# Splitting seven routed down blocks instead of five, with part of the low halves on VectorE

## The reference

```python
topk_idx, topk_w = _router(x, gate_w, e_bias)      # 6 of 32 experts, in 4 of 8 groups
combine = zeros((T, 32)).at[arange(T)[:, None], topk_idx].add(topk_w)
h = square(relu(einsum('th,eih->tei', x, up_w)))   # 32 experts x 64
h = h * combine[:, :, None]
moe_out = einsum('tei,ehi->th', h, down_w)
shared = square(relu(x @ shared_up_w.T)) @ shared_down_w.T
out = x + layernorm(moe_out + shared)
```

## Time and profile before

| | |
|---|---|
| median of 3 runs | 501.53 us (501.43 to 502.6) |
| profiled execution | 502.27 us, its span 500.4 us |
| busy: PE | 460.5 us, 92% |
| busy: DVE | 390.0 us, 78% |
| busy: ACT | 354.2 us, 71% |
| busy: POOL | 248.1 us, 50% |
| mean granted PE clock | 0.989 |

### The profile page before, as it was taken

One profiled execution on the slowest core, in us unless ns is written; L12 is line 12 of the kernel. 1 busy time (PEld: TensorE's weight loads), 2 busy tenths in 40 slices (PEclk: granted clock), 3 DMA queues, 4 the chain that ended last, 5 costly groups with the idle time before them and its releaser, 6 DMA issues.

```text
span 500.4 us, 10661 instructions
## 1 busy us (share of the span) xinstructions
PE 460.5 (92%) x3328; PEld 266.2 (53%) x3328; DVE 390.0 (78%) x1000; ACT 354.2 (71%) x707; POOL 248.1 (50%) x583
## 2 busy tenths in 40 slices
PE   2457999999999999999999899999999999999994
PEld 2212444444444454454456566666666666666662
DVE  3688888899999989989648678695977869496453
ACT  2324788888888888888676677768688776866552
POOL 7045323335757835322733617748293764626351
PEclk9999999999999999999899899999999999999998
DMA  7543344444455445430043344455362545546431
GB/s 207 164 144 102 101 132 133 138 137 143 128 148 151 150 124 151 121 101 3 3 175 126 107 151 133 168 182 182 106 213 87 167 155 189 176 114 207 128 104 42
DMA packets 49047, 67.45 MB, mean 135 GB/s; under 512 B 3808, under 2 KB 35808, under 8 KB 48992
## 3 DMA queue, kind: packets, MB, share of 16 engines
q1 hardware_dynamic: 48992, 66.78, 42.4%
HBM read 51.17 MB, written 15.20 MB: 133 GB/s over the span
## 4 chain that ended last, share of the span: by engine, by line
PE 75%; DVE 10%; issue 7%; POOL 4%; ACT 3%; DMA 0%; POOLq 0%; DVEq 0%; ACTq 0%
PE pO L1295 10%; PE pS L1235 9%; PE pY L1376 8%; PE pS L1376 8%; PE pS L1360 6%; PE pS L1362 6%; PE pS L1361 6%; DVE mneg L953 5%; PE pS L1241 3%; PE pX L1220 2%; PE pY L1312 2%; PE pY L1324 2%; PE pX L1223 2%; DVE q_rest L933 1%; PE pX L1215 1%
## 5 line engine op out<-in xcount | busy, mean ns | idle before, releaser
L953 DVE TENSOR_REDUCE mneg<-pS 128x2 f32<-128x512 f32 x256 | 162.2, 685 | 16.5 <-PE pS L1235 16.1
L742 ACT ACTIVATE probs<-pS 128x512 f32<-128x512 f32 x256 | 141.4, 596 | 26.9 <-PE pS L1241 25.4
L1235 PE MATMUL pS<-qk 48*128 48x256 bf16 x512 | 87.6, 289 | 14.9 <-DVE mneg L953 8.4
L827 ACT ACTIVATE h_ring<-r 128x512 f32<-128x512 f32 x104 | 64.5, 625 | 35.7 <-DVE r L1084 27.4
L1360 PE MATMUL pS<-qk,up_hi 128*128 128x512 f32 x144 | 88.7, 616 | 0.0
L1241 PE MATMUL pS<-qk 51*128 51x256 bf16 x512 | 86.6, 280 | 0.5 <-ACT probs L742 0.3
L1295 PE MATMUL pO<-probs,vv 128*32 128x256 f32 x1024 | 72.9, 392 | 0.0
L1235 PEld LDWEIGHTS pS<-qk 48*128 48x128 bf16 x512 | 33.7, 96 | 65.9 <-DVE mneg L953 44.9
L1084 DVE SCALAR_TENSOR_TENSOR r<-pS,probs 128x512 f32<-128x512 f32 x64 | 43.6, 689 | 29.1 <-PE pS L1362 28.1
L1362 PE MATMUL pS<-qk,up_lo 128*128 128x512 f32 x144 | 57.2, 397 | 0.0
L1361 PE MATMUL pS<-qk,up_hi 128*128 128x512 f32 x144 | 57.0, 396 | 0.0
(11 more groups left out here) (191 smaller groups left out, 819.3 us busy)
## 6 DMA issues: line engine op xcount, KB each, us to landing
c_ring<-c_scratch SPq DMA_DIRECT2D x32, 512.0 KB, 4.0
probs<-c_scratch SPq DMA_DIRECT2D x32, 512.0 KB, 3.9
qk<-qk_scratch SPq DMA_DIRECT2D x64, 192.0 KB
qk_scratch<-q_parts SPq DMA_DIRECT2D x16, 192.0 KB, 2.3
qk_scratch<-k_parts SPq DMA_DIRECT2D x16, 192.0 KB, 2.7
qk_scratch<-q_parts SPq DMA_DIRECT2D x16, 128.0 KB, 2.7
qk_scratch<-k_parts SPq DMA_DIRECT2D x16, 128.0 KB, 2.3
out_x<-probs SPq DMA_DIRECT2D x7, 256.0 KB, 4.7
```

The costliest lines, as they stand in the source:

```text
L742: nc.scalar.activation(probs[j][:, hh], s2_bank(n)[:, :, :], ACT.Exp, scale=SCALE).then_inc(exp_done, 1)
L827: nc.scalar.activation(h_ring[:, (n - at) % HRING], r_sb[n % URING][:, :], ACT.Square).then_inc(sq_done, 1)
L953: nc.vector.tensor_reduce(mneg[u % 2][:, :, hh, k], pS1[n % S1_RING][:, :].rearrange("p (a s) -> p a s", a=TH), AX.X, ALU.max, negate=True ...
L1235: return mm(pS1[n % S1_RING][:, T * th:T * (th + 1)], qp[slot][rows, k, P * th:P * (th + 1)], kp[slot][rows, k, :], start=True, stop=True)
```

## The change

Seven routed blocks are split, every second from 2 to 14. Their high parts use a ring of four (the fourth in a tile that attention has left), the whole ones too. The low parts of blocks 2, 6, 10, 14 are made by POOL, in a ring of two. Those of blocks 4, 8, 12 are made by DVE (`low_h`), in a ring of three of their own, behind the rects of k = 8, 11 and 14 (and behind the routing step of the same k). ACT no longer waits for the low part before it writes the whole square. `split_down` is seven blocks wide.

```diff
-SPLIT = (2, 5, 8, 11, 14)
-SPLIT_LAG, HI_RING, LO_RING = 6, 3, 2
+SPLIT = (2, 4, 6, 8, 10, 12, 14)
+SPLIT_LAG, HI_RING, LO_RING = 6, 4, 2
+
+LOW_AT = {8: 1, 11: 3, 14: 5}
...
+        h_lo2 = unit_tail[1:3]
...
                 if i == 0:
-                    low(i, 1)
                     low(i, 2)
                 if i + 1 < NTILE:
                     root_of_sum(i + 1)
                 if i >= 1:
-                    low(i, 1)
+                    low(i, 2)
                 if i + 2 < NTILE:
                     chain_x1(i + 2)
-                if i >= 1:
-                    low(i, 2)
+                low(i, 4)
                 if i >= 1:
                     chain_f(i - 1)
-                low(i, 3)
-                low(i, 4)
+                low(i, 6)
...
-                    if at >= HI_RING:
-                        act.wait_ge(lo_done, at - HI_RING + 1)
-                    elif at == 1:
+                    if at == 1:
                         act.wait_ge(pv_done, 4 * NB)
...
+            def low_h(i, s):
+                n = FBLK * i + SPLIT[s]
+                at, turn = splits_to(n), PER[1] * i + s // 2
+                dve.wait_ge(hi_done, at + 1)
+                dve.wait_ge(sq_done, n + 1)
+                if turn >= len(h_lo2):
+                    dve.wait_ge(split_done, low_user(1, turn - len(h_lo2)))
+                nc.vector.tensor_tensor(h_lo2[turn % len(h_lo2)], h_whole[at % HI_RING], h_hi[at % HI_RING].bitcast(F32),
+                                        ALU.subtract).then_inc(lo2_done, 1)
...
                     if i + 1 < NTILE and k in ROUTE_AT[i >= 1]:
                         route(rt, i + 1, ROUTE_AT[i >= 1].index(k))
+                    if k in LOW_AT:
+                        low_h(i, LOW_AT[k])
...
-                pe.wait_ge(lo_done, at + 1)
-                high, low = h_hi[at % HI_RING], h_lo[at % LO_RING]
+                turn = PER[s % 2] * i + s // 2
+                pe.wait_ge((lo_done, lo2_done)[s % 2], turn + 1)
+                high, low = h_hi[at % HI_RING], (h_lo, h_lo2)[s % 2][turn % LO_RING]
```

More of the change, by code:

```diff
@@ L201, in block_kernel @@
         spare = probs[4][:, :, :, :].rearrange("p a b c -> p (a b c)")
-        h_whole = [h_ring[:, HRING], spare[:, 0:TILE], spare[:, TILE:2 * TILE]]
-        h_hi, h_lo = ([sb(f"{name}{i}", [P, TILE], F32R)[:, :] for i in range(n)]
-                      for name, n in (("h_hi", HI_RING), ("h_lo", LO_RING)))
+        spare2 = probs[5][:, :, :, :].rearrange("p a b c -> p (a b c)")
+        h_whole = [h_ring[:, HRING], spare[:, 0:TILE], spare[:, TILE:2 * TILE], spare2[:, 0:TILE]]
+        unit_tail = [qk[slot][:, half:half + UB // 2].rearrange("p j a b -> p (j a b)").bitcast(F32R)
+                     for slot, half in ((4, 0), (4, UB // 2), (5, 0))]
+        h_hi = [sb(f"h_hi{i}", [P, TILE], F32R)[:, :] for i in range(HI_RING - 1)] + unit_tail[0:1]
+        h_lo = [sb(f"h_lo{i}", [P, TILE], F32R)[:, :] for i in range(LO_RING)]
+        h_lo2 = unit_tail[1:3]
         down_hi, down_lo = (sb(f"down_{n}", [P, len(SPLIT), D], F32R) for n in ("hi", "lo"))
-        down_whole = down_sb[:, :, :].rearrange("p (a b) d -> p a b d", b=3)[:, 0:len(SPLIT), 0]
+        down_whole = down_sb[:, :, :].rearrange("p (a b) d -> p a b d", b=2)[:, 0:len(SPLIT), 0]
         fT_sb = sb("fT_sb", [P, TILE])
-        assert all(k - SBLK == 3 * s for s, k in enumerate(SPLIT))
+        assert all(k - SBLK == 2 * s for s, k in enumerate(SPLIT))
         assert (HRING + 1) * TILE == RBLK * P and TILE >= SI
@@ L300, in block_kernel @@
         sq_done = sem("sq_done")
-        hi_done, lo_done = sem("hi_done"), sem("lo_done")
+        hi_done, lo_done, lo2_done = sem("hi_done"), sem("lo_done"), sem("lo2_done")
         split_done = sem("split_done")
@@ L332, in splits_to, with low_user @@
             return len(SPLIT) * i + sum(at < k for at in SPLIT)
+        PER = {0: len(SPLIT[0::2]), 1: len(SPLIT[1::2])}
+        def low_user(own, turn):
+            i, s = divmod(turn, PER[own])
+            return len(SPLIT) * i + 2 * s + own + 1
         def part3(eng, wait, b):
@@ L621, in low @@
                 n = FBLK * i + SPLIT[s]
-                at = splits_to(n)
+                at, turn = splits_to(n), PER[0] * i + s // 2
                 pool.wait_ge(hi_done, at + 1)
                 pool.wait_ge(sq_done, n + 1)
-                if at >= LO_RING:
-                    pool.wait_ge(split_done, at - LO_RING + 1)
-                nc.gpsimd.tensor_tensor(h_lo[at % LO_RING], h_whole[at % HI_RING], h_hi[at % HI_RING].bitcast(F32),
+                if turn >= LO_RING:
+                    pool.wait_ge(split_done, low_user(0, turn - LO_RING))
+                nc.gpsimd.tensor_tensor(h_lo[turn % LO_RING], h_whole[at % HI_RING], h_hi[at % HI_RING].bitcast(F32),
                                         ALU.subtract).then_inc(lo_done, 1)
```

## The result

| | before | after |
|---|---|---|
| median | 501.98 us (501.43 to 502.6, 4 runs) | 509.05 us (507.67 to 509.87, 4 runs) |
| profiled execution, its span | 502.27 us, 500.4 us | 507.67 us, 505.8 us |
| busy PE, DVE, ACT, POOL | 460.5, 390.0, 354.2, 248.1 us | 456.9, 406.0, 363.8, 247.7 us |
| mean granted PE clock of the profiled execution | 0.989 | 0.956 |

A forecast was written before the change was run, and what follows sets the result against it. TensorE's own stream was taken to set the pace. Tile 0 +0.8, tiles 1 to 5 +6.3, tiles 6 and 7 -0.7 give +6.4 us: span 506.8, time 507.9 us, range 503.0 to 513.0.

The forecast's parts named there:

- 16 x 0.17: TensorE, two more split down blocks in each of 8 tiles, 0.69 us each against 0.86 whole: 2.7 us less.
- The steps: TensorE's uneven steps in a tile: step 10 starts at 16.38 us and wants block 4's low part at 17.94.
- the wait of 1.6 us: TensorE waiting for VectorE's low part of block 4, 17.94 to 19.54: +1.26 us a tile in tiles 1 to 5.
- The port: VectorE's low part of block 4, blocked by GpSimd's h_lo, ends at h_lo's end plus 0.68 less 0.14: 19.46 us.
- The 28.8 us named for tiles without routing: A sign: the tile takes 30.4 us in tiles 1 to 5 and 28.8 without routing.
- Tile 0: First feed-forward tile, low part 4 behind routing step 5: +0.8 us (+1.9 if L1047 is still slowed), half-clock stretch counted equal.
- the 3.5 named as a sign: TensorE's single wait in tile 0 on the VectorE subtraction, claimed to be near 3.5 us.
- Rival (c): TensorE's waits also bring the clock down, 1.7 us each in two to five tiles: 511.3 to 516.4 us; chance 0.18.
- The sum: Whole kernel: +0.8 +6.3 -0.7 = +6.4 us, span 506.8, time 507.9 us.
- (a): Rival: block 4's low part is there by 17.94, no TensorE wait; -2.7 us, 498.8 us; chance 0.07.
- (b): Rival: VectorE's low part starts before h_lo; wait 0.68 us, +0.34 a tile, 503.3 us; chance 0.13.
- Edits at no cost: ScalarE's added squares, later low parts, GpSimd, DMA, rings and wider split_down: 0 taken, 0.9 us at most for split_down.

The follow-up runs named there:

- at7: Changed kernel with VectorE's low part of block 4 one place earlier, behind rect(7) instead of rect(8): 503.89 us, ratio 1.0036 to the kernel before.
- lag7: Changed kernel with all split downs one step later (lag 7) and f copied at k=3 instead of k=2: 505.63 us, ratio 1.0065 to the kernel before.
- pool_after_dve: Changed kernel with GpSimd's h_lo of block 6 waiting until VectorE's low part of block 4 is done: 506.89 us, ratio 1.0086 to the kernel before.
- the repeated run: The changed kernel once more, nothing edited: 509.86 us (507.46 to 510.21), ratio 1.014 to the kernel before.

## Why the prediction was right

**What bounds the kernel.** Right: TensorE's stream sets the pace. Without VectorE's low parts the kernel got 2.6 us faster, against 2.7 worked out from 16 x 0.17. That the two are so near is in part luck: tiles 1 to 5 gave 0.22 us each and not 0.34, and tile 0 made up for it with a half-clock stretch that isn't there.

**The steps.** Tile 4 begins at 377.63 in the changed kernel. Forecast and measured from there: rect(7) 15.48 and 15.43; end of L1055 15.15 and 15.10; rect(8) 17.26 and 17.22; `h_lo` ends 18.92 and 18.86; TensorE wants the low part at 17.94 and 17.93; it goes on at 19.54 and 19.46. So the wait of 1.6 us is 1.53 by starts. The margin by which GpSimd is first was 0.23 and 0.22. The tile grew by 1.26 us (29.11 to 30.37 over five tiles), forecast 1.26: 6.3 us of the sum. That it was read from starts, not from shares, made this possible: the shares show 5 us in 28 free on VectorE.

**The port.** The low part of block 4 takes 1.59 to 1.60 us in tiles 1 to 5, by the formula (end of `h_lo` plus 0.68 less 0.14) 1.59: 396.49 + 0.54 - 395.44. The rule of the Trainium skill ("SBUF — State Buffer", "SBUF: two separate sides") names exactly this pair, a VectorE operation with two SBUF inputs and a GpSimd operation that reads SBUF, and the trace agrees. The part of the rule on GpSimd operations of any width didn't show for a VectorE operation that starts beside a small one: in tile 6 the low part (455.25) took its 0.68 us in the middle of the pow of 128x4 (454.78 to 455.80), and the tile took 27.35 us, 0.33 less than before, forecast 0.34. (The 28.8 us named for tiles without routing was wrong as a length: tile 6 took 27.68 before.) The other way round it did show: in at7, where VectorE's low part starts 0.14 us ahead of the same pow (391.43, 391.57), the pow takes 1.43 us instead of 1.02.

**Tile 0: the term that was mis-sized.** Forecast +0.8; in the profiled execution tile 0 ended 0.7 earlier, apart from 0.47 us that the attention part brought along. The step up to the end of the wait was right (L1055 takes 0.29 at 274.26; TensorE goes on at 275.63 and is through split 6, at up block 13, by 279.37, where it was at 277.8 before: 1.1 later if 0.47 is taken off, forecast 1.0). But I had counted the half-clock stretch behind it as equal, and it isn't there: 278.15 to 281.57 has a granted clock of 1.00 (the 2.4 GHz level), where it had 0.50. That gives back the 1.7 us, and 1.1 - 0.17 - 1.7 = -0.8 is near the -0.7 measured. The wait of TensorE there is 2.56 us, longer than the 2.10 of before but not near the 3.5 named as a sign: TensorE reached it later, in part because it had stood 0.5 us for ScalarE's `onT` at 270.80. So the length of a wait doesn't settle the clock: lag7 waits only 1.88 us there and has 0.51 from 276 to 278 us, and pool_after_dve has a wait of about the same length as the changed kernel (2.57 us), and its clock fell:

```profile
277.00:280.00 3.00, 3.00 (x10) 2.40 (x9) 2.96 (x8) 1.91 (x4) 2.81 (x7) 0.63 0.42 145
280.00:283.00 3.00, 3.00 (x10) 1.75 (x10) 1.80 (x4) 1.55 (x3) 2.62 (x6) 0.80 0.08 30
```

By the Trainium skill ("TensorE: Matmul & The Clock Gate", "What's actually happening") the gate is driven by recent activity in a window that runs on its own; a difference between two runs with the same wait would fit that, and no run here shows more. Rival (c), that the five waits of 1.4 us bring the clock down, did not come true in any profile of these kernels.

**The sum.** In spans: +0.47 (attention) - 0.73 (tile 0) + 6.32 (tiles 1 to 5) - 0.33 - 0.31 (tiles 6, 7) = +5.4, from 500.4 to 505.8. What the +0.47 comes from stays open: `split_down` is 0.8 us longer, and the granted clock is 0.66 in the first 60 us (1.00 before, with the same 35.9 us of busy TensorE); neither was tested. The medians moved by 7.1. The profiled execution is the fastest of the four of its kernel (507.67 us; median 509.05), and its trace can't say where the others lose 1.4 us. The mean clocks on record give a hint: in the repeated run, of those with a mean near 0.95, the one at 0.956 took 507.46 us and those at 0.951 and 0.950 took 509.95 and 510.21. 0.005 of 508 us is 2.5 us of clock, or 5 us at half clock (an estimate from these means), which would fit a stretch like the one of tile 0 that the two profiled executions lack; no trace of a slower execution shows it. That the 507.9 is within 1.2 us of the median is in part luck: the forecast span, 506.8, is 1.0 above the profiled one, because tile 0 was forecast too long, and the median is above the profiled execution.

**Rivals.** (a), the low part is in time: no. (b), the port doesn't bite: no, but its wait is that of a real kernel: in pool_after_dve, where the low part takes 0.68 us, a wait of 0.63 by starts is left (395.59 + 0.86 to 397.08; 0.47 by the modelled end), where (b) had 0.68. Its time isn't: 506.89 us and not 503.3, as the tile there is 0.7 us longer than before and not 0.34.

**Edits at no cost.** split_down's subtraction took 2.11 us, 0.55 more (forecast 0.6); nothing waited for it. The low parts of blocks 8 and 12 made no wait; in tile 4 they ended at 22.9 and 26.5 us of the tile, ahead of the estimated 24.1 and 27.3, as both took 0.68 us. What I hadn't seen: `low_x` (L1088), untouched by the change, took 1.33 us instead of 0.68 beside the `h_lo` of block 10. It was wanted late enough. A slip in the section on the change: the ring of VectorE's low parts (`unit_tail[1:3]`) holds two, not three; both engines count it by twos, and no number used it.

## What to carry to other kernels

Before work is moved to an engine with free time, read at which microsecond its result will be there and at which it is wanted: 5 us in 28 were free on VectorE, and at the one place that mattered the result was about 0.5 us too late before any contention. Where two engines share a port, the order of two starts 0.05 to 0.2 us apart decides over 0.4 to 1.1 us of the follower, and an edit elsewhere (here one square less on ScalarE) can turn it: list what may run beside each blocked operation, and repair with a wait that fixes the order or with another owner of the work. Taking a wait away seldom gives all of it: 3.0 of 4.5 us were gained in one experiment here, where the moved operation blocked another one, and 6.0 of 7.7 in another, where the engine was late for the next thing.

## What the runs showed of the hardware

- A copy of 128 x 24 in fp32, one operand, takes 1.09 to 1.29 us instead of 0.18 when a GpSimd operation of 1.28 us has begun just ahead of it. The Trainium skill ("SBUF — State Buffer", "Who interferes with whom") lists copies among the operations that can take the shared pair; the traces agree. rect, which reads PSUM, keeps its 0.67 to 0.69 us beside the same operations.
- The order is decided by 0.04 us: GpSimd at 386.89, the copy at 386.93 blocked; GpSimd at 391.30, the copy at 391.25 not. At 0.01 us the recorded starts no longer tell who came first: in tile 4 of pool_after_dve GpSimd's `h_lo` starts at 401.81 and takes 1.84 us, VectorE's `low_x` at 401.82 takes its 0.68.
- It is the one that comes second that waits, GpSimd too: in tile 6 of the changed kernel VectorE's low part of block 8 begins at 459.15 and takes 0.67 us, and GpSimd's `h_lo` at 459.16 takes 1.83 us instead of 1.29, which is again the first one's time less 0.14.
- In tile 0 of four kernels (lag7, before, changed, pool_after_dve), waits of TensorE of 1.88, 2.10, 2.56 and 2.57 us were followed by a granted clock of 0.51 (2 us long), 0.50 (3.4 us), 1.00 (3.4 us) and 0.63 (3 us).
